# An LSTM and a GRU in one pass: sums of squares moved behind the next input product, and one GRU candidate behind the next LSTM product

## The reference

```python
def lstm_step(h, c, x_t):                     # 128 steps
    a = x_t @ Wx + b + h @ Wh                 # 32 x 2048
    i, f, o = sigmoid(a[:, :512]), sigmoid(a[:, 512:1024]), sigmoid(a[:, 1024:1536])
    c = f * c + i * tanh(a[:, 1536:])
    return o * tanh(c), c
x = x + lstm(x, cond)                         # y below
def gru_step(g, y_t):                         # 128 steps, g starts at 0
    z = sigmoid(y_t @ W_z + g @ U_z + cond @ C_z + b_z)
    r = sigmoid(y_t @ W_r + g @ U_r + cond @ C_r + b_r)
    hh = tanh(y_t @ W + (r * g) @ U + cond @ C + b)
    return (1 - z) * g + z * hh
out = x + gru(cond, x)
```

## Time and profile before

| | us |
|---|---|
| median of 3 runs | 1230.14 |
| the three runs | 1230.14, 1232.26, 1229.92 |
| the profiled execution's own time | 1231.91 |
| its span, first to last instruction | 1230.1 |
| PE busy | 1201.3 (98% of the span) |
| DVE busy | 872.3 |
| ACT busy | 445.0 |

### The profile page before, as it was taken

How to read it: one execution, slowest core, us unless ns; L and a number is a source line. 1 busy time by engine, 2 the same in 40 slices (tenths; PEclk the granted TensorE clock), 3 DMA queues, 4 the chain that set the end, 5 groups by cost and what they waited for, 6 DMA issues and landing times.

```text
span 1230.1 us, 68313 instructions
## 1 busy us (share of the span) xinstructions
PE 1201.3 (98%) x31174; PEld 831.7 (68%) x31174; DVE 872.3 (71%) x2681; ACT 445.0 (36%) x1078; POOL 277.7 (23%) x520
## 2 busy tenths in 40 slices
PE   5889999999999999999999999999999999999997
PEld 1467676676676766766767667667676676676765
DVE  2768877777777777777777777777777777777765
ACT  5555233333333333333333333333333333333332
POOL 3100222222222222222222221222222222222221
PEclk9899999999999999999999999999999999999999
DMA  9900100111110011110011111011111001110001
GB/s 307 324 8 9 21 16 9 21 21 21 21 21 8 16 21 20 21 21 12 13 21 21 21 21 19 6 21 21 21 21 21 10 14 21 21 21 12 12 4 29
DMA packets 142066, 39.51 MB, mean 32 GB/s; under 512 B 135825, under 2 KB 136081, under 8 KB 140753
## 3 DMA queue, kind: packets, MB, share of 16 engines
q1 hardware_dynamic: 140080, 34.49, 12.3%
q0 software_dynamic: 640, 0.53, 0.2%
q10 hardware_dynamic: 1056, 0.13, 0.1%
HBM read 26.74 MB, written 8.39 MB: 29 GB/s over the span
## 4 chain that ended last, share of the span: by engine, by line
PE 94%; SPq 3%; DVE 1%; DMA 1%; ACT 1%; issue 0%; DVEq 0%; ACTq 0%
PE ps_l L795 51%; PE ps_g L795 38%; PE ps_g L804 3%; SPq L241 2%; DMA o_area<-in_L_cond_C_dram 1%; PE ps_l L804 1%; SPq L245 1%; ACT o_area L354 0%; DVE u L549 0%; DVE zr L552 0%; SPq L252 0%; SPq L250 0%; PE ps_c L804 0%; ACT zr L468 0%; DVE rgT L730 0%
## 5 line engine op out<-in xcount | busy, mean ns | idle before, releaser
L795 PE MATMUL ps_l<-wx,x2T 128*32 128x512 f16 x6020 | 348.7, 379 | 0.0
L795 PE MATMUL ps_l<-wh,h2T 128*32 128x512 f16 x5952 | 344.5, 379 | 0.0
L795 PEld LDWEIGHTS ps_l<-wx,x2T 128*32 128x32 f16 x6020 | 181.5, 97 | 117.9
L795 PE MATMUL ps_g<-w,y2T 128*32 128x384 f16 x5760 | 256.6, 326 | 0.0
L795 PEld LDWEIGHTS ps_l<-wh,h2T 128*32 128x32 f16 x5952 | 173.2, 97 | 116.7
L795 PEld LDWEIGHTS ps_g<-w,y2T 128*32 128x32 f16 x5760 | 175.4, 97 | 71.2
L328 POOL TENSOR_TENSOR yT<-xT,hT 128x128 f32<-128x128 f32 x128 | 61.7, 482 | 582.4 <-DVE hT L679 582.4
L795 PE MATMUL ps_g<-u,g2T 128*32 128x256 f16 x5760 | 179.8, 273 | 1.0 <-ACT g2T L496 1.0
L795 PEld LDWEIGHTS ps_g<-u,g2T 128*32 128x32 f16 x5760 | 160.2, 97 | 11.2 <-issue 1.4
L552 DVE SCALAR_TENSOR_TENSOR zr<-ps_g,sc,term 128x256 f32<-128x256 f32 x128 | 61.9, 484 | 102.6 <-PE ps_g L795 92.8
L312 POOL TENSOR_TENSOR o_area<-yT,gT 128x128 f32<-128x128 f32 x127 | 58.2, 458 | 297.3 <-DVE gT L778 297.3
(11 more groups left out here) (103 smaller groups left out, 1112.8 us busy)
## 6 DMA issues: line engine op xcount, KB each, us to landing
x_nat<-in_x_dram SPq DMA_DIRECT2D x126, 64.0 KB, 2.6
out_dram<-o_area SPq DMA_DIRECT2D x124, 64.0 KB, 2.1
wh<-in_L_cond_Wx_dram SPq DMA_DIRECT2D x4, 1024.0 KB, 11.1
w<-in_L_cond_Wh_dram SPq DMA_DIRECT2D x3, 1024.0 KB, 18.9
u<-in_L_cond_Wh_dram SPq DMA_DIRECT2D x1, 1024.0 KB, 24.6
stage<-in_L_cond_W_z_dram SPq DMA_DIRECT2D x1, 1024.0 KB, 8.5
stage<-in_L_cond_W_r_dram SPq DMA_DIRECT2D x1, 1024.0 KB, 8.2
stage<-in_L_cond_W_dram SPq DMA_DIRECT2D x1, 1024.0 KB, 10.4
```

The costliest lines, as they stand in the source:

```text
L795: mm = nc.tensor.matmul(bank[B * j:B * j + B, c0:c1].rearrange("p (n c) -> p n c", c=B), still(a, k), moving(b, k, j), start=opens and (a, ...
```

## The change

Two things move in TensorE's list, and nothing is added or removed; the lists of the other engines are the same.

- The `squares` of the GRU's weights (W and U) in tick 4 stood behind the LSTM's product of that tick. They now stand behind the product of x for tick 5, ahead of `bound`.
- The candidate's product of GRU step 1 stood at the end of tick 2. It now stands in tick 3, behind the LSTM's product of that tick, its fourth. Those of the other steps stay.

```diff
+            def candidate_as_given(s):
+                pe.wait_ge(rgT_done, s)
+                if s == 1:
+                    pe.wait_ge(u1_in[2], 16)
+                gate_as_given(ps_g[s % 2], 2, rgT, u_raw[2], range(K), False, True).then_inc(cand_ps, 1)
+
             def tick(t, n, i):
...
                     pe.wait_ge(wh_squares, K)
                     squares(K, K)
                     bound(1, 1)
-                if t == T_WU_SCALE:
-                    pe.wait_ge(w1_squares, GG)
-                    pe.wait_ge(u1_squares, GG)
-                    squares(2 * K, 2 * GG)
+                if t == LAG + 2:
+
+                    candidate_as_given(1)
 
                 m = t - 1
...
                     product(ps_l[(t + 1) % NL], 0, GL * P, wx_of, x_of((n + 1) % U // Q, (n + 1) % Q), 0, END, True, False)
+                if t == T_WU_SCALE:
+                    pe.wait_ge(w1_squares, GG)
+                    pe.wait_ge(u1_squares, GG)
+                    squares(2 * K, 2 * GG)
                 if q == 0 and 0 < group < NG - 1:
                     bound(1 - r, group + 1)
                 if t >= T - 1:
                     go_on(7)
-                if recurs and s < F:
-                    pe.wait_ge(rgT_done, s)
-                    if s == 1:
-                        pe.wait_ge(u1_in[2], 16)
-                    gate_as_given(ps_g[s % 2], 2, rgT, u_raw[2], range(K), False, True).then_inc(cand_ps, 1)
-                elif recurs:
+                if recurs and 1 < s < F:
+                    candidate_as_given(s)
+                elif recurs and s >= F:
                     if s == F:
```

## The result

The changed kernel takes 1228.77 us in the median of 11 runs (1227.6 to 1229.58); the kernel before, run beside it, 1231.19 us (11 runs, 1229.92 to 1232.7). The ratio is 0.998, with a 95% interval of 0.997 to 0.9989: 2.4 us less, between 1.4 and 3.7.

A forecast was written before the change was run, and what follows sets the result against it. PE bounds the kernel, busy 98% of the span. The squares' 4.18 us gain less the candidate's 0.69 us loss gives 3.49, so 1231.9 - 3.5 = 1228.4 us (1228.3 from the median), range 1226.5 to 1230.4.

The forecast's parts named there:

- The place: PE before 85 us: time can come only from its two holes, 1.74 us for `rgT` and 2.30 us for ScalarE's sum.
- The candidate's move costs: Ticks 2 and 3: moving step 1's candidate starts the product of g 0.69 us later, a loss taken alone.
- the candidate's sum 1.93 late: DVE, tick 3: its candidate sum starts at 66.57 instead of 64.64, and the work queued behind it is late too.
- a new hole for `gT`: PE, tick 3: a wait of 1.27 us opens behind the product of y, ahead of the product of g.
- The squares' move gains: Ticks 4 to 5: from the end of the LSTM's product to the next one's start, 8.15 us instead of 12.33, 4.18 less.
- the split of the 4.18 into a hole of 2.49 and a clock of 1.69: Tick 4: 2.49 us from the removed wait ahead of the squares, 1.69 from products no longer slowed by the clock.
- Sum: PE, tick 5: the LSTM's product starts at 86.18 instead of 89.67, 3.49 us earlier, kept to the end.
- The step that failed: Tick 4: only some executions have the low clock, so the median run gains 2.49 - 0.69 = 1.80 us.
- The way over the median: Whole kernel: the median of 1230.1 us less 1.8 gives 1228.3 us.
- The way over the profiled execution: Whole kernel: the profiled execution's 1231.9 us less 3.5 gives 1228.4 us.
- The first rival: Tick 4: the median already holds the low clock, so it too loses 3.5 us, to 1226.6; chance 0.16.
- The rivals with new low-clock stretches: Ticks 2 and 3: the clock drops behind one new hole (1230.1 us, chance 0.14) or both (1231.8 us, 0.04).

The follow-up runs named there:

- the half sum: Kernel before in its old order, with U's last sum of squares over 1024 of its 2048 columns: 1229.64 us, ratio 0.9986.
- before again: Kernel before, run once more unchanged: 1231.20 us, ratio 1.0003.
- candidate only: Kernel before with just the candidate's product of GRU step 1 moved, squares at their old place: 1232.23 us, ratio 1.0009.
- refilling only VectorE's queue: Changed kernel with DVE's two low halves of Wh moved ahead of the candidate's sum, ScalarE's list as it was: 1227.98 us, ratio 0.9975.
- the second run with both queues refilled: Changed kernel with DVE's two low halves of Wh and ScalarE's second sum of squares of W moved earlier, run again: 1226.72 us, ratio 0.996.

## Why the prediction was right, and where it was not

- **The place.** That only two holes of PE before 85 us were in play was right: the 1134.15 us from tick 5 on stayed the same to 0.01.
- **The candidate's move costs.** Foretold 0.69, measured 0.75 (16.57 - 15.82), in the changed kernel and alone. Each link showed: restart on `hT` (1.16 us of hole, as foretold), the candidate's sum 1.93 late (measured 1.96 from the product of g on), a new hole for `gT`. The last was foretold from starts at 1.27, and is 70.60 - 66.68 - 2.62 = 1.30 by starts; the 1.12 in the row counts from the modelled end of the product before.
- **The squares' move gains.** Foretold 4.18, measured 14.92 - 10.89 = 4.03. The step that was mis-sized is the price of products back to back around the squares: the product of x before them took 85.50 - 82.79 = 2.71 instead of 2.59, the squares 0.31 instead of 0.29, the bound 0.04 instead of 0.02. Of the split of the 4.18 into a hole of 2.49 and a clock of 1.69, the half sum bore out the clock's part: 1.66 came back beside the 0.86 by which the hole was shorter.
- **Sum.** 3.49 foretold, 3.28 measured in the distances. The profiled execution began its product of g of tick 2 0.34 later, so its LSTM's product of tick 5 is 2.94 earlier, and the span 3.3 shorter with a last store that took a little less.
- **The step that failed** is "I read this as the low clock behind the second hole coming in some executions only. Then the median run has lost only the hole". Every profile with the 2.3 us hole had the low clock (before, before again, candidate only), and the mean clocks say that about nine in ten executions have it. The spread is mostly the start-up's, and the median of 1230.14 was simply a low one of three; with 11 it is 1231.19.
- **Luck.** That the same end came out both ways, 1228.3 and 1228.4 against 1228.77 measured, is in part luck. The way over the median took 1.69 too little off a median that was 1.05 too low. The way over the profiled execution started from a time 0.7 above the median of 11. From that median the sum would have given 1231.19 - 3.49 = 1227.70, 1.1 below what was measured. The first rival had the cause right, that the median holds the low clock; its 1226.6 was too low because it started from the low median of three.
- **The rivals with new low-clock stretches** did not come: at 1.16 and 1.12 us of hole in ticks 2 and 3, as at 1.74 there and at 1.45 in tick 4, the clock stayed at 1.00 in every profile.
- **What stays open.** The distances say 3.28 us, the medians 2.4 (1.4 to 3.7 by the interval). Nor is it this pair alone. In the eight runs of kernels without the low clock the median fell short of what the distances say by 0.00 to 1.14 us, 0.71 on average, and never went beyond it, which looks like more than chance. Executions of the kernel before that escape the low clock would explain this, but it would take about four in ten of them (0.71 of 1.7), and the mean clocks speak for about one. What the rest is, no run here shows.

## What to carry to other kernels

A wait costs the engine not only its length: here 2.3 us of idle TensorE were followed by a stretch at 1.2 GHz worth another 1.7, so a hole near that size is worth removing first, and shortening it (by 0.86 us here) was enough in the one kernel that tried it. Moving one product behind another in TensorE's queue helps only if what waits for it on the other engines has nothing long queued behind: here 0.58 us of earlier start became 0.75 of loss, and refilling only VectorE's queue handed the wait on to the next tile. A change of two parts should be priced part by part: here the better kernel leaves the candidate's move out, or mends the queues behind it. Where the start-up makes executions differ by over a microsecond, compare distances between two fixed instructions of the trace; the median of three runs is no evidence on what one execution holds.

## What the runs showed of the hardware

In ticks 2 to 4 the full clock survived idle stretches of TensorE of 1.74 us in every profile that had one (five) and one of 1.45 us, and fell behind 2.30 and 2.31 us in all three. There it fell only after PE had been busy again for more than a microsecond. The windows of PE in the kernel before, where PE had restarted at 79.83:

```profile
81.00:81.20 0.20, 0.20 (x16) 1.00 0.00 0
81.20:81.40 0.20, 0.20 (x14) 0.75 0.00 0
```

The clock falls between 81.2 and 81.4, some 1.5 us after the restart; in the kernel before, once more, it does so between 81.8 and 82.0, some 1.2 us after its restart at 80.69. The Trainium skill (TensorE: Matmul & The Clock Gate, Part 1) says that the monitor runs free of the kernel's start; the traces agree, in that the start of the low clock moved against the restart from one profile to another.

That it falls after the restart is no rule, though. In the start-up of the same trace of the kernel before, the clock fell while PE was still idle, near 47.2, in a hole of 2.46 us that ended at 47.57 (the window, then the timeline):

```profile
47.00:47.20 0.20, 0.00 (x0) 0.92 1.11 430
```

```profile
47.57 1.93 PE L804 MATMUL ps_c<-u,h0T 128*32 128x128 f32 x32 [2.46 <-DMA u<-in_L_cond_C_r_dram]
```

And in the start-up of the second run with both queues refilled it fell at about 48.2, 0.7 us behind a hole of 2.08 us, so a wait a little under 2.3 us has been enough there. Waits of 0.74 and 1.16 us stand on either side of it, and the first may count too; no run here parts that.

The 14.92 us of the second distance were the same to the hundredth in all three profiles with the hole, which fits a stretch that lay whole within the products behind the hole each time. That sameness was not expected.
